# A two-layer gated cross-attention kernel: layer 0 projected once a batch, its stacks taken through a scratch in HBM

## The chip, the cores and the metric

One core of a Trainium2 chip runs the whole kernel in one launch. The metric is the device time of one execution in microseconds (us). The kernel before took 320.93 us, the median of 3 runs (319.45 to 321.24).

## What is computed

x is 2 batches of 256 tokens of 128 values, ctx is 2 batches of 512 tokens of 128 values. Four residual steps, each gated by a tanh of a learned number:

```
x = x + tanh(g_xattn[0]) * attention0(layernorm(x), ctx)   # 16 heads of 8, shared mask
x = x + tanh(g_ffn[0])   * quantised_linear(layernorm(x))  # x @ Hadamard, 4 bit, ternary weights
x = x + tanh(g_xattn[1]) * attention1(layernorm(x), ctx)   # 16 heads of 64, mask by batch
x = x + tanh(g_ffn[1])   * moe(layernorm(x))               # 32 experts, top 4, one shared expert
```

Each attention projects queries, keys and values, takes a masked softmax of the scores over 512 keys, mixes the values and projects out. All inputs are float32, and the scores must keep float32 accuracy. The router picks experts by rank, so small errors upstream matter. That is why queries and keys are split into a high part and a low remainder, and products of both parts are added up.

## The kernel before, in words

**Units, blocks and slots.** A unit is one head and 128 queries of one batch: a 128x512 tile of scores. Layer 0 has 8 blocks (2 batches x 4 groups) of 8 units (4 heads x 2 query tiles); layer 1 has 16 blocks (2 batches x 8 groups) of 4 units. Units are numbered 0 to 127. Every engine runs the same written order over slots t from -6 to 129, each its own part: TensorE computes in slot t the scores of unit t+6, then the jobs planned for t, the mix and output projection due in t, and turns (transposes) unit t; VectorE masks unit t+5, takes the reciprocal of unit t+3, evicts the jobs of slot t-1 and copies half of the turned tiles; ScalarE takes the exponential of unit t+4 and copies the other half; GpSimd normalises unit t+3. There is no reordering: an instruction that waits holds up all behind it on its engine. From slot 130 the experts follow.

**Jobs.** `make_plan` (line 105) says in which slot a projection or another piece of side work is issued, `BEFORE` what comes ahead of slot -6. Jobs take two PSUM banks in turn, and a job waits until the last user of its bank was evicted (`freed`).

**Layer 0's projections.** Each of the 8 blocks projects its own k (L991), q (L988) and values (L995). The weights are laid out so that 32 columns, four heads of 8, stand four times over the 128 output rows. One eviction on ScalarE (L577) and one on VectorE (L762) leave the high parts in some row groups and the low parts in the others, so that one matmul over 128 rows (L1057) adds all four products. The k stack is then ready. The q stack is copied once per head by GpSimd (`q_stack`, L453 to L460), multiplied by 1 in the rows of that head and by 0 in the others. Values are copied into 8 of every 32 columns (L735).

**Mix and output.** When a block's 8 units are turned, TensorE mixes them with the values (L1089) into `mix_bank`, ScalarE copies it with its bias (L556), and two matmul pairs (L1101) add it into `y_bank`. That is once for each of the 8 blocks.

**The feed-forward's chain** (`feed_forward`, L812) starts when a batch's last output projection is in, at slot `Y_DONE[0, b]` (37 and 69), and goes through all engines in steps o = 0 to 17 behind that slot: residual add, statistics, 1/sqrt on GpSimd, normalise, turn (o = 4), rotate (7), quantise (9, 10), turn (11), linear (13), add (14), statistics, normalise, turn (17). Layer 1's first q (slot 55 for batch 0) needs its result. The weights' ternary form (`ternary`, nine VectorE operations) is made in slots -4 to -2.

**Layer 1's stacks.** k and q of a block are stacked by DMAs from SBUF to SBUF that SyncE issues in plan order (`stack_k` L395, 4 DMAs; `stack_q` L403, 6 DMAs), each pair behind the slot of its projection. Scores of layer 1 (L1063, L1064) wait for them. SyncE also loads the experts' weights there (L424).

**Loads.** All inputs are loaded at the start, SyncE's in the order of L378 to L391.

Of the kernel before, what the change touches and what calls it, by code (L numbers as in the profile page):

```python
# [53 lines left out]
for _name, _n in (("bq0", 4), ("bk0", 4), ("bq1", 8), ("bk1", 8), ("gates", 4), ("lo_k", 1), ("lo_q", 1),  # L54
                  ("head_row", 4), ("neg_half", 4), ("bv0", 4), ("bv1", 8)):
    COL[_name], NCOLS = slice(NCOLS, NCOLS + _n), NCOLS + _n
# [48 lines left out]
def make_plan():  # L105


    before = [("k", 0), ("ln", 0, 0), ("q", 0), ("v", 0)]
    plan = {}
    ahead = ({"k": 13, "q": 11, "v": 10}, {"k": 13, "q": 11})  # L110
    for k in BLOCKS[1:]:
        for name, slots in ahead[k.layer].items():
            if name == "q" and k.layer == 1 and k.g == 0:
                slots = 9
            plan.setdefault(k.first - slots, []).append((name, k.m))
# [3 lines left out]
    plan.setdefault(4, []).append(("turn_fw",))  # L119
# [19 lines left out]
    for j in order:  # L139
        if j[0] in ("k", "q"):  # L140
            count += 1
            highs[j] = count
# [19 lines left out]
PIECES_FROM = 14  # L162

# [12 lines left out]
def build(nc, a, out):  # L176
    ctx = ExitStack()
    with ctx:
# [21 lines left out]
        head_row, gates = cols[:, COL["head_row"]], cols[:, COL["gates"]]  # L200
# [5 lines left out]
        ctxT = sb("ctxT", [P, NC * P])  # L206
# [25 lines left out]
        w0T = shared[:, 0:2048].rearrange("p (g i c) -> p g i c", g=4, i=4)  # L232
        stack_f = shared[:, 2048:2304]
        mask0 = shared[:, 2304:2816].bitcast(BF16).rearrange("p (t k) -> p t k", t=NQ)
        we3 = shared[:, 0:HALVES * P].rearrange("p (e c) -> p e c", e=HALVES)
        parts = sb("parts", [P, 3840], F32R)
        q0 = parts[:, 0:2048].rearrange("p (i h q) -> p i h q", i=2, h=4)
        k0 = parts[:, 2048:3072].rearrange("p (i k) -> p i k", i=2)
        high_k, high_q = parts[:, 3072:3584], parts[:, 3584:3840]
        w1_late = parts[:, 0:3072].rearrange("p (g n i c) -> p g n i c", g=4, n=2, i=3)  # L240
        gateT = parts[:, 3072:3584]
        minus_bq0 = sb("minus_bq0", [P, 4])
        minus_bk0 = sb("minus_bk0", [P, 4])
        bo0 = sb("bo0", [P, P])
        m0_u8 = sb("m0_u8", [P, NQ, SK], U8)
# [13 lines left out]
        k1_both = sb("k1_both", [P, NKQ, 2, SK], F32R)  # L259
# [985 lines left out]
```

## Time and profile before

| | us |
|---|---|
| median of 3 runs | 320.93 |
| the profiled execution | 321.6 |
| its span, first to last instruction | 319.9 |
| TensorE busy | 281.8 (88%) |
| VectorE busy | 226.1 (71%) |
| ScalarE busy | 197.6 (62%) |
| GpSimd busy | 132.9 (42%) |

The profile records one execution. PE is TensorE, PEld its weight loads, DVE VectorE, ACT ScalarE, POOL GpSimd, SP SyncE; SPq is a DMA issue on SyncE. L12 is line 12 of the kernel. Times are us from the span's start. Ends of matmuls are modelled, so starts are the better measure: the cost of a TensorE instruction in a busy stretch is the start of the next one less its own.

### The profile page before, as it was taken

To read this page: it belongs to the slowest core of one execution; us is meant where nothing else is said; L and a number is where in the kernel's file an instruction comes from. 1 tells how busy PE (TensorE), PEld (TensorE's weight loads), DVE (VectorE), ACT (ScalarE), POOL (GpSimd) and SP (SyncE) were. 2 spreads that over 40 slices of the span, in tenths; PEclk is the share of its full clock that TensorE was granted. 3 is DMA by queue.
4 is the path that set the end of the run, shared out by engine and by line. 5 is a ranking of instruction groups with operands and counts; after the bars stand their busy time and mean duration, and the time that the engine had idled before them with its cause. 6 is when DMAs were issued, how large, how long until landed. Compare 5 with 4: busy or idle time off the path is not lost.

```text
span 319.9 us, 6774 instructions
## 1 busy us (share of the span) xinstructions
PE 281.8 (88%) x1963; PEld 218.1 (68%) x1963; DVE 226.1 (71%) x713; ACT 197.6 (62%) x475; POOL 132.9 (42%) x209
## 2 busy tenths in 40 slices
PE   2649799999778759999999999999999789989996
PEld 0426476677466537688877788888787558777995
DVE  1489887897785956788789677797786117376653
ACT  1258698898685756797776666676967642613221
POOL 4436768876775552748453233343244000000000
PEclk9999999999997998999999999999999799979999
DMA  6900000000000253545456367665620000000000
GB/s 186 395 6 1 3 0 2 4 0 1 3 0 2 66 121 95 141 116 127 115 143 172 95 157 203 172 179 152 169 59 3 0 2 1 0 2 16 1 2 16
DMA packets 17124, 23.43 MB, mean 73 GB/s; under 512 B 3264, under 2 KB 10944, under 8 KB 16960
## 3 DMA queue, kind: packets, MB, share of 16 engines
q1 hardware_dynamic: 16656, 22.64, 25.7%
q10 hardware_dynamic: 432, 0.35, 0.6%
q8 instruction: 17, 0.28, 0.4%
q14 instruction: 19, 0.16, 0.1%
HBM read 8.04 MB, written 0.26 MB: 26 GB/s over the span
## 4 chain that ended last, share of the span: by engine, by line
PE 57%; DVE 17%; issue 10%; ACT 5%; DMA 4%; POOL 3%; SPq 3%; DVEq 0%; ACTq 0%; POOLq 0%
PE bank L1089 13%; PE bank L951 12%; PE bank L1131 4%; PE bank L1152 4%; PE bank L1155 4%; DVE masked L705 4%; PE bank L1063 3%; PE bank L1064 3%; PE bank L1057 2%; POOL probs L451 2%; SPq L409 2%; PE bank L1101 2%; DVE probsT L721 2%; DMA q<-q_split 2%; PE bank L956 2%
## 5 line engine op out<-in xcount | busy, mean ns | idle before, releaser
L451 POOL TENSOR_SCALAR probs<-probs,rsum 128x512 f32<-128x512 f32 x128 | 88.4, 695 | 104.8 <-DVE rsum L714 104.2
L540 ACT ACTIVATE probs<-masked,neg_max 128x512 f32<-128x512 f32 x128 | 91.8, 719 | 7.2 <-DVE neg_max L705 7.2
L951 PE MATMUL bank<-ident,probs 128*128 128x128 f32 x512 | 79.7, 279 | 3.3 <-ACT probsT L548 1.7
L951 PEld LDWEIGHTS bank<-ident,probs 128*128 128x128 f32 x512 | 59.4, 143 | 22.7 <-issue 13.7
L705 DVE CUSTOM_DVE_ANT_0 masked<-bank,mask 128x512 f32<-128x512 f32 x64 | 43.7, 683 | 17.0 <-PE bank L1064 13.9
L548 ACT ACTIVATE probsT<-bank 128x512 f32<-128x512 f32 x74 | 43.7, 591 | 17.8 <-PE bank L951 17.7
L1089 PE MATMUL bank<-probsT,val 128*32 128x256 f32 (+1 forms) x512 | 49.4, 405 | 1.3 <-ACT mixT L556 1.3
L721 DVE COPY probsT<-bank 128x512 f32<-128x512 f32 x54 | 36.7, 679 | 19.3 <-PE bank L951 19.2
L705 DVE CUSTOM_DVE_ANT_0 masked<-bank,shared 128x512 f32<-128x512 f32 x64 | 43.3, 678 | 1.4 <-PE bank L1057 1.2
L1089 PEld LDWEIGHTS bank<-probsT,val 128*32 128x32 f32 (+1 forms) x512 | 25.6, 128 | 21.0 <-issue 8.9
L1057 PE MATMUL bank<-parts 128*128 128x512 f32 x64 | 31.1, 492 | 8.7 <-issue 6.5
L651 ACT ACTIVATE probsT<-bank 128x256 f32<-128x256 f32 x34 | 13.0, 385 | 36.9 <-PE bank L1152 36.9
L1063 PE MATMUL bank<-k_high,q 128*128 128x512 f32 x64 | 30.5, 477 | 3.9 <-DMA q<-q_split 3.9
L935 DVE TENSOR_TENSOR probsT<-bank,probsT 128x256 f32<-128x256 f32 x32 | 13.6, 424 | 22.3 <-PE bank L1155 11.1
L1064 PE MATMUL bank<-k_both,q 128*128 128x512 f32 x64 | 25.2, 394 | 0.0
L540 ACT ACTIVATION_READ_ACCUMULATOR probs<-masked,neg_max 128x1 f32 x128 | 24.9, 194 | 0.0
L556 ACT ACTIVATE mixT<-bank,cols 128x256 f32<-128x256 f32 x24 | 11.3, 472 | 17.4 <-PE bank L1089 17.3
L1131 PE MATMUL bank<-we,probsT 128*128 128x128 f32 x136 | 21.2, 280 | 0.1
L714 DVE RECIPROCAL rsum<-sums 128x1 f32<-128x1 f32 x128 | 19.9, 156 | 1.7 <-ACT probs L540 1.7
L1057 PEld LDWEIGHTS bank<-parts 128*128 128x128 f32 x64 | 12.4, 195 | 12.8 <-issue 11.8
L1152 PE MATMUL bank<-xnT,w_flat 128*128 128x256 f32 x68 | 20.9, 390 | 0.0
L1155 PE MATMUL bank<-xnT,shared 128*128 128x256 f32 x68 | 20.8, 388 | 0.0
(166 smaller groups left out, 470.9 us busy)
## 6 DMA issues: line engine op xcount, KB each, us to landing
q<-q_split SPq DMA_DIRECT2D x96, 64.0 KB, 2.0
k_both<-k_low SPq DMA_DIRECT2D x32, 128.0 KB, 2.9
k_both<-k_high SPq DMA_DIRECT2D x32, 128.0 KB, 3.2
w_flat<-in_w SPq DMA_DIRECT2D x1, 1536.0 KB, 9.7
shared<-in_w0T SPq DMA_DIRECT2D x1, 768.0 KB, 7.1
w_flat<-in_we SPq DMA_DIRECT2D x2, 384.0 KB, 3.6
shared<-in_we SPq DMA_DIRECT2D x2, 384.0 KB, 4.2
we<-in_we SPq DMA_DIRECT2D x2, 384.0 KB, 4.4
```

The source lines that it names most:

```text
L451: pool.tensor_scalar(p, p, rsum[:, u % NCOL:u % NCOL + 1], 1.0, ALU.mult, ALU.mult).then_inc(normed, 1)
L540: act.activation(probs[:, u % NP, :], masked[:, u % NS, :], ACT.Exp, scale=-1.0, bias=neg_max[:, c:c + 1], accum_out=sums[:, c:c + 1]).the ...
L548: act.activation(probsT[:, k.m % 2, h, :, qt * P:qt * P + P], turn_bank[u % 2][:, :].rearrange("p (k q) -> p k q", q=P), ACT.Copy).then_in ...
L705: dve.tensor_tensor_reduce(out=masked[:, u % NS, :], in0=score_bank[u % 2][:, :], in1=mask, scale=-float(k.depth) ** -0.5, scalar=3.0e38, ...
L721: dve.tensor_copy(probsT[:, k.m % 2, h, :, qt * P:qt * P + P], turn_bank[u % 2][:, :].rearrange("p (k q) -> p k q", q=P)).then_inc(copied[ ...
L951: ins = pe.transpose(dst[0:rows, t * P:t * P + P], src, ident[:, :])
L1057: pe.matmul(dst, q0[:, i, h, q], k0[:, i, :], start=True, stop=True).then_inc(scored, 1)
L1063: pe.matmul(dst, q1_high[:, s, h, q], k1_high[:, s, :], start=True, stop=False)
L1064: pe.matmul(dst, q1_both[:, s, h, q], k1_both[:, s, h, :], start=False, stop=True).then_inc(scored, 1)
L1089: ins = pe.matmul(mix_bank[w * h:w * h + w, 0:SQ], v[:, i, w * h:w * h + w], probsT[:, k.m % 2, h, i, :], start=(i == 0), stop=(i == NK - 1))
L1131: ins = pe.matmul(moe_bank[b][:, t * P:t * P + P], hidT[:, n % 2, t * P:t * P + P], we2[:, p, :], start=(p == 0 and t == 0), stop=(p == PA ...
L1152: pe.matmul(u_bank[i][:, 0:SQ], we1[:, p, :], xT, start=True, stop=True).then_inc(u_ready, 1)
```

## The change

- **Layer 0 is projected once a batch.** New jobs `kn`, `qn` and `v0` project all 16 heads in one go: one k, q and value projection for each batch. The split is as in layer 1: high part by ScalarE, low part by VectorE. Block 0 alone is still projected in the repeated layout (from `w00T`), so that it needs no DMA; its q is put into the four heads' tiles by four VectorE operations on 32 partitions each, in place of GpSimd's `q_stack`.
- **Stacks go through HBM.** SyncE writes the high and low parts to `staged_k` and `staged_q` in HBM, each row twice, waits, and reads them back as the stacks of blocks 1 to 7: one DMA for k and four for q in each block. Rows now alternate high and low inside a head. There are four stack buffers in place of two, cleared once by GpSimd.
- **Mixes are summed over groups.** The values of group g stand in the columns of g, zeros elsewhere, and the four blocks of a batch add into one `mix_bank`. Copy and output projection come once a batch.
- **The chain takes 15 steps**: residual add and statistics in o = 0, normalise 2, turn 3, rotate 5, quantise 7 and 8, turn 9, linear 11, add 12, statistics 13, normalise 14, turn 15. Layer 1's first q of each batch comes two slots sooner (53 and 85).
- **Moved**: the ternary weights to slots 11 to 13 (turned in 18, before 4), the loads of layer 1 behind the stacks of blocks 1 to 3. Layer 1's q stack takes 4 DMAs (a repeated source) in place of 6. Expert loads wait also for the context's split, since the context now lies in `shared`.

```diff
-    before = [("k", 0), ("ln", 0, 0), ("q", 0), ("v", 0)]
-    plan = {}
-    ahead = ({"k": 13, "q": 11, "v": 10}, {"k": 13, "q": 11})
-    for k in BLOCKS[1:]:
-        for name, slots in ahead[k.layer].items():
-            if name == "q" and k.layer == 1 and k.g == 0:
-                slots = 9
-            plan.setdefault(k.first - slots, []).append((name, k.m))
+    before = [("k", 0), ("kn", 0), ("ln", 0, 0), ("q", 0), ("qn", 0)]
+    plan = {1: [("v0", 0)]}
+    for k in BLOCKS[8:]:
+        plan.setdefault(k.first - 13, []).append(("k", k.m))
+        plan.setdefault(k.first - 11, []).append(("q", k.m))
+    for n, name in enumerate(("kn", "qn", "v0")):
+        plan.setdefault(LN01_AT + 7 + n, []).append((name, 1))
-        for o, job in ((4, ("ln", 1, b)), (7, ("rotate", b)), (11, ("turn_xq", b)), (13, ("ffn", b)),
-                       (17, ("ln", 2, b))):
+        for o, job in ((3, ("ln", 1, b)), (5, ("rotate", b)), (9, ("turn_xq", b)), (11, ("ffn", b)),
+                       (15, ("ln", 2, b))):
...
+            def stage_k0(b):
+                sp.wait_ge(*freed(("kn", b)))
+                for low, src in ((0, k1_high[:, b, :]), (1, k1_low[:, b, :])):
+                    sp.dma_start(staged_k[b, :, low::2, :].bitcast(F32),
+                                 src.bitcast(F32).unsqueeze(1).to_broadcast([P, 2, SK])).then_inc(k_staged[b], 16)
+                sp.wait_ge(k_staged[b], 32)
+
+            def stage_q0(b):
+                sp.wait_ge(*freed(("qn", b)))
+                for low in range(2):
+                    sp.dma_start(staged_q[b, :, 2 * low:2 * low + 2, :].bitcast(F32),
+                                 q1_split[:, b, low, :].bitcast(F32).unsqueeze(1).to_broadcast([P, 2, SQ])).then_inc(q_staged[b], 16)
+                sp.wait_ge(q_staged[b], 32)
+
+            def stack_k0(k):
+                i, c = k.m % 4, 32 * k.g
+                if k.m >= 4:
+                    sp.wait_ge(scored, BLOCKS[k.m - 4].end)
+                sp.dma_start(k0[:, i, :].bitcast(F32),
+                             staged_k[k.b, c:c + 32, :, :].bitcast(F32).rearrange("c j k -> (c j) k")).then_inc(stacked0[i], 16)
+
+            def stack_q0(k):
+                i, c = k.m % 4, 32 * k.g
+                if k.m >= 4:
+                    sp.wait_ge(scored, BLOCKS[k.m - 4].end)
+                for h in range(4):
+                    sp.dma_start(q0[32 * h:32 * h + 32, i, h, :].bitcast(F32),
+                                 staged_q[k.b, c + 8 * h:c + 8 * h + 8, :, :].bitcast(F32)
+                                 .rearrange("c j q -> (c j) q")).then_inc(stacked0[i], 16)
+
+            stage_k0(0)
+            for k in BLOCKS[1:4]:
+                stack_k0(k)
+            stage_q0(0)
+            sp.wait_ge(late_ready, 2)
+            for k in BLOCKS[1:4]:
+                stack_q0(k)
             sp.dma_start(m1_u8[:, :, :, :], a["mask1"]).then_inc(ld["m1"], 16)
             sp.dma_start(w1_flat[:, :], a["w1"]).then_inc(ld["w1"], 16)
...
+            stage_k0(1)
+            stage_q0(1)
+            for k in BLOCKS[4:8]:
+                stack_k0(k)
+                stack_q0(k)
...
-                    for copy in range(2):
-                        sp.dma_start(q1[own[h], s, h, copy, :].bitcast(F32),
-                                     q1_split[own[h], i, 0, :].bitcast(F32)).then_inc(q_stacked[s], 16)
+                    sp.dma_start(q1[own[h], s, h, :, :].bitcast(F32),
+                                 q1_split[own[h], i, 0, :].bitcast(F32).unsqueeze(1).to_broadcast([64, 2, SQ])).then_inc(q_stacked[s], 16)
...
+                            sp.wait_ge(ctx_split, 2 * B)
...
+                        for h in range(4):
+                            r = slice(32 * h, 32 * h + 32)
+                            ins = dve.scalar_tensor_tensor(out=q0[r, 0, h, :], in0=job_bank[r, 0:SQ], scalar=bq00[r, 0:1],
+                                                           in1=high_q[r, :].bitcast(F32), op0=ALU.add, op1=ALU.add)
+                            ins.then_inc(q0_ready if h < 3 else free, 1)
...
+                    else:
+                        pe.wait_ge(stacked0[k.m % 4], 80 * turns_of_stack0(k.m))
+                    pe.matmul(dst, q0[:, k.m % 4, h, q], k0[:, k.m % 4, :], start=True, stop=True).then_inc(scored, 1)
...
-                                        probsT[:, k.m % 2, h, i, :], start=(i == 0), stop=(i == NK - 1))
+                                        probsT[:, k.m % 2, h, i, :], start=(first and i == 0), stop=(last and i == NK - 1))
...
-                if t in (-4, -3, -2):
-                    ternary(t + 4)
+                if t in (11, 12, 13):
+                    ternary(t - 11)
```

## Rows read from the trace of the kernel before

**Rows 1.** The page's busy line: us, share of the span, instructions.

```profile
PE 281.8 (88%) x1963; PEld 218.1 (68%) x1963; DVE 226.1 (71%) x713; ACT 197.6 (62%) x475; POOL 132.9 (42%) x209
```

**Rows 2.** Stretches: from:to, length, busy us of each engine, granted clock, DMA share, GB/s.

```profile
25.80:76.10 50.30, 47.25 (x376) 33.88 (x375) 42.59 (x144) 41.46 (x104) 37.19 (x62) 1.00 0.01 2
60.05:70.90 10.85, 10.60 (x93) 7.75 (x96) 9.19 (x32) 9.25 (x24) 8.40 (x15) 1.00 0.01 2
76.10:110.50 34.40, 26.84 (x202) 19.44 (x201) 28.06 (x98) 24.73 (x61) 21.05 (x33) 0.95 0.07 16
110.50:117.50 7.00, 3.63 (x24) 2.97 (x24) 4.72 (x14) 4.61 (x11) 5.26 (x8) 1.00 0.27 66
117.50:133.80 16.30, 15.82 (x114) 12.03 (x118) 11.45 (x34) 10.30 (x25) 6.80 (x11) 0.90 0.51 122
192.00:200.00 8.00, 8.00 (x59) 6.42 (x58) 6.01 (x18) 5.56 (x14) 2.91 (x5) 1.00 0.75 202
```

**Rows 3.** TensorE's timeline, unit 8 and a steady block: start, us, what.

```profile
25.78 0.47 PE L1057 MATMUL bank<-parts 128*128 128x512 f32 x1
...
49.12 1.93 PE L1089 MATMUL bank<-probsT,val 128*32 128x256 f32 x32
...
51.71 1.02 PE L991 MATMUL bank<-ctxT,shared 128*128 128x512 f32 x2
52.57 0.60 PE L951 MATMUL bank<-ident,probs 128*128 128x128 f32 x4
...
55.58 1.05 PE L995 MATMUL bank<-shared,ctxT 128*128 128x128 f32 x8
56.47 0.60 PE L951 MATMUL bank<-ident,probs 128*128 128x128 f32 x4
```

**Rows 4.** VectorE's timeline in that block.

```profile
51.67 0.69 DVE L721 COPY probsT<-bank 128x512 f32<-128x512 f32 x1 [1.24 <-PE bank L951]
...
58.80 0.67 DVE L705 CUSTOM_DVE_ANT_0 masked<-bank,shared 128x512 f32<-128x512 f32 x1
...
59.47 0.67 DVE L721 COPY probsT<-bank 128x512 f32<-128x512 f32 x1
60.05 0.68 DVE L705 CUSTOM_DVE_ANT_0 masked<-bank,shared 128x512 f32<-128x512 f32 x1
```

**Rows 5.** Groups of VectorE instructions: busy us, mean ns, then idle before.

```profile
L762 DVE SCALAR_TENSOR_TENSOR parts<-bank,cols,parts 128x512 fp32r<-128x512 f32 x8 | 6.0, 749 | 4.4 <-ACT parts L577 3.8 <-PE bank L1057 0.6
L762 DVE SCALAR_TENSOR_TENSOR shared<-bank,cols,parts 128x256 f32<-128x256 f32 x8 | 3.8, 472 | 2.5 <-ACT parts L577 2.5
L735 DVE COPY val<-bank 128x128 f32<-128x128 f32 x8 | 2.2, 272 | 0.6 <-PE bank L995 0.6
L799 DVE TENSOR_REDUCE fcol<-fw 128x1 f32<-128x128 f32 x1 | 0.3, 276 | 0.0
L810 DVE TENSOR_TENSOR fq<-fw,fs 128x128 f32<-128x128 f32 x1 | 0.5, 450 | 0.0
```

**Rows 6.** The start, TensorE's and GpSimd's timelines.

```profile
6.38 2.04 PE L991 MATMUL bank<-ctxT,shared 128*128 128x512 f32 x2 [6.38 <-DMA ctxT<-in_ctxT]
...
13.80 1.84 POOL L459 TENSOR_SCALAR parts<-shared,cols 128x256 fp32r<-128x256 f32 x4 [4.11 <-DVE shared L762]
```

**Rows 7.** DMAs (KB, us to landing), then layer 1's first q stack and the waits.

```profile
q<-q_split SPq DMA_DIRECT2D x96, 64.0 KB, 2.0
out<-x_sb SPq DMA_DIRECT2D x2, 128.0 KB, 1.8
...
115.32 0.60 SPq L411 DMA_DIRECT2D q<-q_split  x1
...
117.48 0.47 PE L1063 MATMUL bank<-k_high,q 128*128 128x512 f32 x1 [2.98 <-DMA q<-q_split]
...
118.11 3.19 PE L1089 MATMUL bank<-probsT,val 128*32 128x256 f32 x32
...
133.08 0.47 PE L1063 MATMUL bank<-k_high,q 128*128 128x512 f32 x1 [0.48 <-DMA q<-q_split]
```

More of the change, by code:

```diff
@@ L162, with mixes, turns_of_stack0 @@
 PIECES_FROM = 14
+VALUES_AT = {4: (0, (0, 1, 2, 3)), 20: (1, (0,)), 22: (1, (1,)), 29: (1, (2,)), 37: (1, (3,))}
+def mixes(k):
+    return k.b + 1 if k.layer == 0 else k.m - 5
+def turns_of_stack0(m):
+    return m // 4 + (1 if m % 4 else 0)
 def turns_of_stack(m):
@@ L278, in build @@
         lr = sb("lr", [P, NQ])
-        ex = sb("ex", [P, NQ, EXPERTS])
-        sc = sb("sc", [P, NQ, EXPERTS])
         top8 = sb("top8", [P, NQ, 8])
-        above = sb("above", [P, NQ, EXPERTS])
-        equal = sb("equal", [P, NQ, EXPERTS])
-        run = sb("run", [P, NQ, EXPERTS])
         room = sb("room", [P, NQ])
-        sel = sb("sel", [P, NQ, EXPERTS])
         sel_b = sb("sel_b", [P, NT, EXPERTS], BF16)
-        kept = sb("kept", [P, NQ, EXPERTS])
-        wgt = sb("wgt", [P, NQ, 2, EXPERTS])
+        ex, sc, above, equal, run, sel, kept = (small[:, 64 * i:64 * i + 64].rearrange("p (t e) -> p t e", t=NQ) for i in range(7))
+        wgt = small[:, 4 * P - 64:5 * P - 64].rearrange("p (t i e) -> p t i e", t=NQ, i=2)
         ones32 = sb("ones32", [P, EXPERTS])
@@ L336, in build @@
         ctx_split = sem("ctx_split")
+        k_staged = [sem("k_staged0"), sem("k_staged1")]
+        q_staged = [sem("q_staged0"), sem("q_staged1")]
+        stacked0 = [sem(f"stacked0_{i}") for i in range(4)]
+        val_ready = sem("val_ready")
         w1_split = sem("w1_split")
@@ L451, in norm @@
                 pool.tensor_scalar(p, p, rsum[:, u % NCOL:u % NCOL + 1], 1.0, ALU.mult, ALU.mult).then_inc(normed, 1)
-            def q_stack(m):
-                pool.wait_ge(*freed(("q", m)))
-                if m >= 2:
-                    pool.wait_ge(scored, BLOCKS[m - 2].end)
-                for j in range(4):
-                    pool.tensor_scalar(q0[:, m % 2, j, :], stack_f[:, :], head_row[:, j:j + 1], 1.0,
-                                       ALU.mult, ALU.mult).then_inc(q0_ready, 1)
             splits = [0]
@@ L494, in _ @@
                     norm(t + LEAD - 3)
-                for job in PLAN.get(t - 1, ()):
-                    if job[0] == "q" and BLOCKS[job[1]].layer == 0:
-                        q_stack(job[1])
+                if t in VALUES_AT:
+                    b, groups = VALUES_AT[t]
+                    for g in groups:
+                        values(b, g)
                 if t in SPLIT_AT:
@@ L621, in attend @@
                 for k in BLOCKS:
-                    if t == k.copy_at:
+                    if t == k.copy_at and (k.layer or k.g == 3):
                         mix_copy(k)
@@ L1076, in mix @@
                 if k.layer == 0:
-                    pe.wait_ge(*freed(("v", k.m)))
-                    v = val[:, k.m % NV, :, :]
+                    pe.wait_ge(val_ready, k.m + 1)
+                    v = val[:, k.g, :, :]
+                    first, last = k.g == 0, k.g == k.groups - 1
                 else:
@@ L1083, in mix @@
                     v = val1[:, two % NV1, :, odd * P:odd * P + P]
-                if k.m >= 1:
-                    pe.wait_ge(mix_copied, k.m)
+                    first = last = True
+                if first and k.m:
+                    pe.wait_ge(mix_copied, mixes(k) - 1)
                 w = k.width
@@ L1118, in attend @@
                         mix(k)
-                    if t == k.out_at:
+                    if t == k.out_at and (k.layer or k.g == 3):
                         project_out(k)
```

249 lines of the change are left out of this document (138 added, 111 removed).

## The prediction

> **What bounds the kernel now.** The kernel works in slots t: in slot t TensorE computes the scores of unit t+6 and turns unit t, VectorE masks unit t+5, and each engine keeps its written order. I read the page's busy line first [rows 1]: TensorE is busy 88% of the span, VectorE 71%. That is a mean over unlike stages, so the second view is the table of stretches [rows 2]. In a steady block of layer 0 (60.05 to 70.90, 8 units in 10.85 us) TensorE is busy 10.60 and VectorE 9.19, so TensorE ends it. In the stretch with batch 0's feed-forward chain (76.1 to 110.5) TensorE is busy only 26.84 of 34.4 and VectorE 28.06: there the chain, which is mostly VectorE work, ends it, and TensorE waits in order. In layer 1 (192 to 200) TensorE is busy 8.00 of 8.00. The change touches layer 0 and the chain, so only the time up to about 117 us and two small waits behind it can move.
>
> Third comes TensorE's timeline of one block [rows 3]. Behind each row the reader subtracts its start from that of the next instruction. One k projection costs 0.86 (51.71 to 52.57), the values 0.89 (55.58 to 56.47), the mix 1.9 by its own duration. I put q, with half of k's columns, at 0.43 and an output projection, half as many matmuls as the values, at 0.44; both are estimates. Fourth is VectorE's timeline [rows 4]: mask plus reciprocal take 0.67 (58.80 to 59.47), a turned copy 0.58 (59.47 to 60.05). With a copy in every other unit that is 0.96 a unit, 7.7 a block. The copy at 51.67 waited 1.24 behind the mix, once a block. So without the projections VectorE (7.7 plus 1.2) and TensorE (10.60 less 2.6 of jobs) are both near 8 to 9: VectorE is what is late next.
>
> **The change, part by part.** All sums run against the profiled execution (321.6 us, span 319.9 and 1.7 around it). The median of the runs is 0.7 lower.
>
> A, the start. Before, scores of unit 8 (block 1, slot 2) start at 25.78 [rows 3]. After, block 1 needs its stack from the scratch. The first k pair of matmuls took 2.04 from 6.38 [rows 6]; the new full k projection is another such pair, to 10.5; its eviction on ScalarE (about 0.7) and its low part on VectorE (0.75, like the parts row of [rows 5]) free it at 12.0. Then SyncE issues, in order: two staging DMAs of k (1.05 MB in sum, each row written twice), waits for them, three k stacks (0.79 MB), two staging DMAs of q (0.52 MB), waits, and four q stacks before block 1 is complete. An issue takes 0.6 and a small transfer lands 2.0 after its issue begins [rows 7]. For the rate the nearest row is 192 to 200: 202 GB/s at a DMA share of 0.75 [rows 2], so 270 GB/s full. k is staged at 12.0 + 2.0 + 3.9 = 17.9; q behind the k stacks at 17.9 + 2.0 + 4.9 = 24.8; the fourth q stack starts at 26.6 and lands at 28.6. Scores of unit 8 start at 29.0: **+3.2**. Bounds: at 202 GB/s it is 32 (+6); if bytes cost nothing the stack lands at 22.8 and VectorE's eight masks end near 22 as well, so 23 (-3). I take 270, since these packets are like the ones in that row. What is queued behind SyncE's two waits are the mask and weight loads of layer 1. The mask is wanted in slot 12 and the weights in slot 22 at the earliest, 10 us and more after they are issued at about 32. The first query's four heads were four GpSimd operations (1.84 in all from 13.80 [rows 6]); now they are four VectorE operations on 32 partitions, 0.4 to 0.47 each by the q row of [rows 5]. Mask 0 starts some 0.7 later, inside A's wait. GpSimd's memsets grow by about 1.8 us and lie ahead of its first normalisation: nothing.
>
> The Trainium skill (DMA: Bandwidth & Descriptors, Anatomy of one DMA) speaks against A: a fixed cost of about 2.0 us per DMA, mostly the receipt of the last write, "surprisingly long" where the target is HBM, plus bytes at 436 GB/s. Our only writes to HBM are the two stores of the result, and they landed in 1.8 us against 2.0 for SBUF to SBUF [rows 7], so the trace shows the fixed part and no surcharge. By the page's two figures unit 8 would start about 1.5 us earlier than by mine.
>
> B, slots 2 to 37 (before 25.8 to 76.1, 50.3 us). VectorE was busy 42.6. It loses five k (0.75), four q (0.47) and five v copies (0.27) [rows 5], 7.0 in sum; it gains the full k and q low parts of batch 1 (0.75 + 0.47), two value copies of a full bank (0.68 each, as the copy rows of [rows 4]), and the nine ternary operations moved from slots -4 to -2 into 11 to 13 (3.2; first and last of nine in [rows 5]), 5.8 in sum. That leaves 41.4 busy. Four mixes at 1.24 of idle each give 46.4: **-3.9**. Below, TensorE's own sum would allow 38; above, nothing saved. I take VectorE's sum, the later of the two. The ternary move costs its 3.2 here because A's wait would have covered it and slot 11 doesn't. GpSimd loses 32 operations of 0.49 for eight small copies, ScalarE five k and five q evictions and three mix copies: both were no bound.
>
> Batch 1's stack: its k is projected in slot 13 (about 44), freed at 46, and by A's path with one k stack in place of three it lands near 60. Block 4 is wanted in slot 26, near 62. Slack 2 us: taken as nothing, and the first thing to go.
>
> C, the chain (slots 37 to 55, 34.4 us; after 37 to 53). VectorE's busy 28.06 loses the jobs of the two blocks in it (one k, two q, two v: 2.2) and two slots at 0.96 (1.9): 23.9. Its idle time of 6.3 loses the two waits of 0.6 for k's eviction: 5.1. Together 29.0: **-5.4**. The chain's steps themselves (quantise, normalise) are untouched, about 10 us on VectorE. Bounds: -2.2 if the cut slots only stretch the others, -8 if the idle time goes too.
>
> D, from q to the first scores of layer 1. Before 7.0 us over three slots, TensorE busy 3.63 [rows 2]: SyncE issued six DMAs, the last at 115.32, and TensorE idled 2.98 [rows 7]. After there are four, and five slots. DMAs alone: 1.7 to the first issue, 1.8, 2.0, so 5.5; five slots take about 6.5. **-0.5**, the stall turned into work that C already counts. Bounds -1.5 and +1.
>
> E, the clock. In the 16.3 us behind that stall the granted clock is 0.90 [rows 2], and the mix took 3.19 against 1.93 in the steady block [rows 3, 7]. Without the stall that is **-1.2**. The new idle stretch in A will bring such a dip too, but VectorE sets the pace there. The Trainium skill (TensorE: Matmul & The Clock Gate, HAM oscillation) has the same rule, idle gaps bring the half rate back; by it A's gap is the one to fear, and with half-rate work for one mix behind it the sum would be 1.2 higher.
>
> F, layer 1. Two more waits for q stacks, 0.48 at 133.08 [rows 7] and the like at 183; the first has four DMAs in place of six, batch 1's q comes two slots (4 us) sooner. **-0.9**, bounds 0 and -1.5. The expert loads now also wait for the context's split in slot 80, which holds SyncE up for up to three slots, while block 15's stack is wanted in slot 86: nothing.
>
> Sum: 3.2 - 3.9 - 5.4 - 0.5 - 1.2 - 0.9 = -8.7, so 312.9 beside 321.6, and **312.2** beside the median.
>
> **The rivals.** R1, TensorE stays the bound throughout. For: it was, in steady blocks [rows 2]. Behind unit 8 it loses five k, five q, five v and six output projections: 4.3 + 2.2 + 4.5 + 2.6 = 13.6. This takes the place of B and C: 3.2 - 13.6 - 0.5 - 1.2 - 0.9 = -13.0, near 308. Against: VectorE's sum in B, and TensorE's idle 7.6 us in the chain.
>
> R2, the three engines hand one another too many short waits once none has slack, and half of B, C, E and F is lost while A and D stand: 3.2 - 5.7 - 0.5 = -3.0, near 318. For: between 25.8 and 76.1 TensorE, the bound, was still idle for 3 us (47.25 busy of 50.3) [rows 2]. Against: six units of lead.
>
> R3, the other side: the scratch is the new wait. If the path from freed k to complete stack takes x longer than my 17 us, A grows by x and block 4's wait by x - 2. The change is slower from 2x - 2 > 8.7, x above 5.4. At x = 9 it costs +7.3, near 328. For: nothing in the trace stores 1 MB to HBM or reads it back at once; two waits stand in one queue. Against: loads at the start land fast and the two stores in 1.8 us.
>
> R4, the shorter chain doesn't do what it says: the same work in fewer slots just makes each slot longer, and C gives -3.5. Near 314, inside the forecast's range.
>
> **How the numbers follow.** Forecast (with R4) 0.59, R1 0.15, R2 0.17, R3 0.09. R1 and the forecast are faster by over 0.5% (1.6 us, about what a measurement of this kernel can tell from no change); R2 nearly always, 0.14 of its 0.17; R3 splits 0.01 same, 0.08 slower. Faster 0.88, same 0.04, slower 0.08. The range runs from 306 (R1, with A's lower bound in part) to 319 (R2).
>
> **What would show it.** A: scores of unit 8 at 27 to 32, with an idle TensorE ahead of them waiting for a DMA. B: a steady block near 8.9 us instead of 10.85, VectorE the busiest. C: 28 to 31 us from the first residual add to q of layer 1. D, E: no 3 us wait before layer 1's first scores, the mix behind it under 2 us. F: those two waits gone. The prediction is wrong if unit 32 waits for its stack, if a steady block stays over 10 us, or if the stretch behind 133 moves by more than 2 us.

## The result and the profile after

| | before | after |
|---|---|---|
| median, us (range, runs) | 321.09 (319.45 to 323.26, 4) | 310.87 (309.31 to 311.81, 4) |
| ratio to before, 95% interval | 1 | 0.9673 (0.9603 to 0.9743) |
| profiled execution, us (span) | 321.6 (319.9) | 310.97 (309.2) |
| granted clock, mean | 0.979 | 0.972 |

The changed kernel is 10.2 us faster; 312.2 was predicted, range 306 to 319. The same kernel, timed again later (e12), gave 311.05 (6 runs), ratio 0.9708 (0.9663 to 0.9753). Ratios leave out executions over 1.5% above the fastest of their kernel, medians keep them, so the two can differ by some thousandths.

The page's busy line of the kernel after, beside [rows 1]: TensorE lost 13.3 us of work, VectorE 2.2.

```profile
PE 268.5 (87%) x1871; PEld 206.8 (67%) x1871; DVE 223.9 (72%) x700; ACT 190.1 (61%) x459; POOL 124.3 (40%) x187
```

Stretches of the kernel after, columns as in [rows 2]. In order: unit 8 to the first residual add (50.30 us before, 47.35 now), a steady block (10.85, now 8.90), the chain (34.40, now 28.40), q to the first scores of layer 1 (7.00, now 7.20), and the piece behind them, whose clock was 0.90 and is 1.00. The mean clock column of the first and the third line is below 1.00: TensorE ran at its lower level for a part of them. In the steady block VectorE (7.10) and TensorE (8.40) both have gaps; neither is full.

```profile
25.95:73.30 47.35, 41.17 (x323) 28.69 (x323) 40.12 (x139) 35.26 (x88) 29.95 (x50) 0.96 0.38 125
60.30:69.20 8.90, 8.40 (x73) 5.78 (x72) 7.10 (x25) 6.46 (x18) 5.14 (x9) 1.00 0.36 97
73.30:101.70 28.40, 20.68 (x166) 15.25 (x163) 24.37 (x85) 20.02 (x51) 16.82 (x25) 0.94 0.00 1
101.70:108.90 7.20, 5.03 (x34) 4.17 (x34) 6.63 (x21) 6.67 (x18) 5.36 (x9) 1.00 0.68 147
108.90:122.50 13.60, 13.60 (x109) 10.75 (x109) 10.70 (x31) 8.96 (x22) 7.70 (x11) 1.00 0.65 142
```

TensorE's timeline of the kernel after, the instructions that answer to [rows 3] and [rows 7] and those with the longest waits (in brackets, with their releaser). Unit 8 starts at 25.95, as before, but behind a DMA; unit 32 (59.92) waits for its stack; the first scores of layer 1 still wait 1.67; and in layer 1 there is a new wait of 1.38 at batch 1's turned query (149.40).

```profile
25.95 0.66 PE L1134 MATMUL bank<-parts 128*128 128x512 f32 x1 [2.26 <-DMA parts<-staged_q]
...
59.92 0.47 PE L1134 MATMUL bank<-parts 128*128 128x512 f32 x1 [1.24 <-DMA parts<-staged_q]
60.32 1.93 PE L1168 MATMUL bank<-probsT,val 128*32 128x256 f32 x32
...
101.68 0.35 PE L1024 MATMUL bank<-x_high,w_early 128*128 128x256 f32 x1 [1.23 <-DVE x_low L813]
108.88 0.47 PE L1140 MATMUL bank<-k_high,q 128*128 128x512 f32 x1 [1.67 <-DMA q<-q_split]
109.51 1.93 PE L1168 MATMUL bank<-probsT,val 128*32 128x256 f32 x32
...
131.51 0.50 PE L1140 MATMUL bank<-k_high,q 128*128 128x512 f32 x1 [0.70 <-DVE neg_max L767]
136.96 0.44 PE L1019 MATMUL bank<-ident,xn 128*128 128x128 f32 x2 [0.38 <-DVE k_low L843]
149.40 0.41 PE L1019 MATMUL bank<-ident,xq 128*128 128x128 f32 x2 [1.38 <-DVE xq L862]
```

Where the 10.7 us between the two profiled spans went. A milestone is the start of a unit's scores or of a slot's mix, read from the two TensorE timelines.

| stretch | before | after | difference | forecast |
|---|---|---|---|---|
| start to unit 8 | 25.78 | 25.95 | +0.2 | +3.2 |
| unit 8 to scores of slot 37 | 49.98 | 47.33 | -2.6 | -3.9 |
| to q of layer 1 | 34.8 | 28.4 | -6.4 | -5.4 |
| to unit 64 | 6.95 | 7.20 | +0.2 | -0.5 |
| to the mix of slot 66 | 16.2 | 13.6 | -2.6 | about -1.5 |
| to the mix of slot 94 | 59.8 | 61.7 | +1.9 | about -0.5 |
| to the end | 126.4 | 125.0 | -1.4 | 0 |

The forecast's E (-1.2) and F (-0.9) are spread over the last three lines.

### The profile page after: what moved, and what is told of

Its sections match the earlier page's. It is cut to its first block, busy times and chain, and to the rows that moved or that the text cites. A ratio compares the mean times of both kernels' runs of the same rounds, so it can differ in the third digit from the quotient of the medians.

```text
span 309.2 us, 6506 instructions
## 1 busy us (share of the span) xinstructions
PE 268.5 (87%) x1871; PEld 206.8 (67%) x1871; DVE 223.9 (72%) x700; ACT 190.1 (61%) x459; POOL 124.3 (40%) x187
## 4 chain that ended last, share of the span: by engine, by line
PE 59%; DVE 14%; DMA 9%; issue 7%; ACT 5%; POOL 3%; SPq 3%; DVEq 0%; ACTq 0%; POOLq 0%
PE bank L1019 13%; PE bank L1168 12%; PE bank L1212 5%; PE bank L1233 4%; PE bank L1140 4%; PE bank L1236 4%; PE bank L1141 4%; DMA staged_q<-q_split 3%; DMA staged_k<-k_low 3%; PE bank L1024 2%; PE bank L1134 2%; PE bank L1026 2%; PE bank L1025 2%; PE bank L1181 2%; PE bank L1242 2%
## 5 line engine op out<-in xcount | busy, mean ns | idle before, releaser
L1019 PE MATMUL bank<-ident,probs 128*128 128x128 f32 x512 | 80.8, 282 | 2.9 <-DVE probsT L783 1.3
L1019 PEld LDWEIGHTS bank<-ident,probs 128*128 128x128 f32 x512 | 60.9, 144 | 19.8 <-issue 9.3
L1168 PE MATMUL bank<-probsT,val 128*32 128x256 f32 (+1 forms) x512 | 46.6, 384 | 1.3 <-ACT mixT L616 1.3
L1134 PE MATMUL bank<-parts 128*128 128x512 f32 x64 | 33.5, 529 | 11.9 <-DVE neg_max L767 7.9
L1168 PEld LDWEIGHTS bank<-probsT,val 128*32 128x32 f32 (+1 forms) x512 | 24.6, 123 | 19.3 <-issue 5.2
L1003 DVE TENSOR_TENSOR probsT<-bank,probsT 128x256 f32<-128x256 f32 x32 | 13.6, 424 | 21.8 <-PE bank L1236 11.5
L1134 PEld LDWEIGHTS bank<-parts 128*128 128x128 f32 x64 | 13.1, 206 | 18.2 <-DVE neg_max L767 13.4
L1212 PEld LDWEIGHTS bank<-we,probsT 128*128 128x128 f32 x136 | 18.7, 196 | 0.7 <-DVE probsT L1008 0.3
```

The source lines that it names most:

```text
L1019: ins = pe.transpose(dst[0:rows, t * P:t * P + P], src, ident[:, :])
L1134: pe.matmul(dst, q0[:, k.m % 4, h, q], k0[:, k.m % 4, :], start=True, stop=True).then_inc(scored, 1)
L1168: ins = pe.matmul(mix_bank[w * h:w * h + w, 0:SQ], v[:, i, w * h:w * h + w], probsT[:, k.m % 2, h, i, :], start=(first and i == 0), stop=( ...
L1212: ins = pe.matmul(moe_bank[b][:, t * P:t * P + P], hidT[:, n % 2, t * P:t * P + P], we2[:, p, :], start=(p == 0 and t == 0), stop=(p == PA ...
```

## The experiments

Ratios are to the kernel before, with 95% intervals; the changed kernel stands at 0.9673 and 0.9708. The edit of e3 is made to the kernel before, all others to the changed kernel. No run puts layer 0's projections back into the changed kernel, so what they are worth by themselves is read from the traces and not tried.

**The chain: 17 steps again, in both batches and in batch 1 only; and 15 steps in the kernel before.** `LONG` is (0, 1) in e1 and (1,) in e2; the projection of the batch's first q moves back with it. e3 is the reverse edit on the kernel before.

```diff
-        for o, job in ((3, ("ln", 1, b)), (5, ("rotate", b)), (9, ("turn_xq", b)), (11, ("ffn", b)),
-                       (15, ("ln", 2, b))):
+        for o, job in (((4, ("ln", 1, b)), (7, ("rotate", b)), (11, ("turn_xq", b)), (13, ("ffn", b)),
+                        (17, ("ln", 2, b))) if b in LONG else
...
-                if o in (7, 8):
-                    quantise(b, o - 7)
+                q_at = 9 if long else 7
+                if o in (q_at, q_at + 1):
+                    quantise(b, o - q_at)
```

> The changed kernel with the feed-forward's chain back at 17 steps in both batches, everything else as changed. Theory: in layer 0 the 15-step chain saves about two slots (2 us) between the residual add and q of layer 1, but in layer 1, where slots take 2 us anyway, it only makes TensorE wait in order for VectorE (1.38 us ahead of the turn of xq, 0.38 ahead of the layernorm turn), some 2 us. So undone in both batches it is about even: 310 to 312, with scores of unit 64 near 111 (after 108.9) and layer 1's blocks from slot 66 to 94 in 60 us in place of 61.7. Rival: the shorter chain is worth its two slots in both batches; then 314 to 315.

> The changed kernel with the chain at 17 steps for batch 1 alone. Theory: keeps layer 0's gain and takes back layer 1's loss: 309 (2 us under the changed kernel's 310.9), unit 64 still at 108.9, no wait over 0.5 us ahead of the turn of xq near 150. Rival: layer 1's loss has nothing to do with the chain's steps (the denser stacks, the clock): then 311, and the wait for the q stack of block 16 comes back for 0.5 us more.

> The kernel before with the 15-step chain alone. Theory: in layer 0 it saves two slots and the 3 us wait ahead of unit 64 (3 to 4 us at unit 64: 114), and loses 2 us in layer 1: near 319. Rival: as VectorE still has the projections' evictions, the slots only stretch and nothing is saved in layer 0: 321 to 323.

Measured: e1 311.98, 0.9677 (0.9648 to 0.9706); e2 308.59, 0.9573 (0.9546 to 0.9600); e3 322.39, 1.0010 (0.9972 to 1.0048). So the cut as a whole is worth nothing that can be measured: e1 equals the changed kernel, and e3 came out as its rival said. It costs in batch 1. Mix of slot 66 to mix of slot 94, first the kernel before, then e3, e1 and e2, each from its own trace:

```profile
133.70:193.50 59.80, 59.02 (x432) 46.30 (x431) 48.28 (x148) 42.17 (x102) 29.61 (x46) 1.00 0.54 138
```

```profile
134.60:196.20 61.60, 59.00 (x432) 46.26 (x431) 48.22 (x147) 42.35 (x102) 29.59 (x46) 1.00 0.53 137
```

```profile
123.30:182.90 59.60, 59.09 (x434) 46.35 (x433) 48.96 (x151) 42.78 (x104) 29.89 (x46) 1.00 0.59 142
```

```profile
123.20:182.40 59.20, 58.89 (x432) 46.28 (x431) 48.87 (x151) 42.84 (x104) 29.89 (x46) 1.00 0.59 143
```

And the changed kernel:

```profile
122.40:184.10 61.70, 59.13 (x432) 46.30 (x431) 48.89 (x151) 43.08 (x104) 30.06 (x46) 1.00 0.58 137
```

TensorE's work is 59 us in all five. With 17 steps it is idle for 0.3 to 0.8 in sum; with 15, for 2.6. The three waits at 131.51, 136.96 and 149.40 (2.46 together) are that: TensorE reaches its turns before VectorE has masked, quantised and split. In e3 the same wait stands in the kernel that has nothing else of the change:

```profile
161.48 0.41 PE L950 MATMUL bank<-ident,xq 128*128 128x128 f32 x2 [1.38 <-DVE xq L793]
```

Batch 0 is less clear. Between e1 and e2, which differ only there, the times differ by 0.0104 of 321, 3.3 us, but the profiles reach unit 64 together (109.73 and 109.68; e2 was expected at 108.9) and slot 94 within 0.4; most of the rest of their spans' difference (309.5 and 307.4) lies in the last stretch, where e1 had a clock of 0.90 between 229.6 and 247.4. From the mix of slot 34 to unit 64, the changed kernel, then e1, then e2:

```profile
69.20:108.90 39.70, 29.81 (x247) 22.46 (x246) 34.07 (x116) 29.67 (x76) 25.08 (x38) 0.96 0.13 28
```

```profile
68.10:109.70 41.60, 31.38 (x246) 22.05 (x245) 33.95 (x116) 30.28 (x77) 25.27 (x38) 0.96 0.11 25
```

```profile
68.10:109.70 41.60, 32.21 (x247) 24.50 (x246) 34.30 (x116) 29.64 (x76) 24.74 (x37) 0.88 0.12 25
```

Here e1 and e2 are equally long for different reasons. In e2 TensorE's work slows between 78.48 and 81.91 (four turned tiles 1.06 in place of 0.60, scores 0.77 in place of 0.48), behind a wait of 1.46; the changed kernel has the same wait and doesn't slow. That block takes e2 13.76 (68.15 to 81.91) and the changed kernel 12.13 (69.22 to 81.35). In three more profiles with 15 steps in batch 0 the stretch takes 40.4 (e12), 39.7 (e5b) and 39.6 (e6b). So batch 0's cut gains 1 to 2 us in its own stretch where the clock doesn't take it back, on the strength of one profile with 17 steps. In the kernel before the stretch takes 46.6 at a clock of 0.96, and 48.0 with 15 steps at 0.89, so that pair doesn't speak against it. One profile of each kernel doesn't tell what gave e2's 3.3 us.

**The scratch: everything stored twice, one after the other.** In e4 each staging stores first to a spare scratch and waits for it.

```diff
             def stage_k0(b):
                 sp.wait_ge(*freed(("kn", b)))
+                for low, src in ((0, k1_high[:, b, :]), (1, k1_low[:, b, :])):
+                    sp.dma_start(spare_k[b, :, low::2, :].bitcast(F32),
+                                 src.bitcast(F32).unsqueeze(1).to_broadcast([P, 2, SK])).then_inc(spare[b], 16)
+                sp.wait_ge(spare[b], 32)
```

> The changed kernel with each staging of k and q done once more ahead, into a spare scratch, with its wait. Theory: the way through HBM is on the path at unit 8 and at unit 32 (TensorE waited 2.26 and 1.24 us there): k's second staging adds about 4 us and q's about 4 to 5, so unit 8 moves from 25.95 to about 34 and unit 32 waits another 8: 325 to 328. Rival: VectorE has work in store behind the wait and makes up most of it; then 313 to 318.

Measured: 327.74, 1.0170 (1.0134 to 1.0205): slower than the kernel before. Two waits in e4's TensorE timeline, units 8 and 32:

```profile
33.80 0.77 PE L1146 MATMUL bank<-parts 128*128 128x512 f32 x1 [8.79 <-DMA parts<-staged_q]
...
74.99 0.77 PE L1146 MATMUL bank<-parts 128*128 128x512 f32 x1 [8.17 <-DMA parts<-staged_q]
```

Unit 8 is 7.9 us later, and unit 32 another 7.2 on top of that (15.1 against 59.92). Nothing hides the path to the scratch, in either batch: R3's mechanism is real. By an estimate from these numbers (a gain of 10.2 us, two batches) the change would be worth nothing with each round trip some 5 us longer; e4's are 7 to 8 us longer.

**The query's staging ahead of the wait for the key's.** e5b issues both stagings before it waits for either.

```diff
             def stage_k0(b):
...
-                sp.wait_ge(k_staged[b], 32)
...
+            stage_q0(0)
+            sp.wait_ge(k_staged[0], 32)
```

> The changed kernel with q's staging issued as soon as q is free, ahead of the k stacks and of the wait for k's staging, in both batches. Theory: unit 8 waits for the q stack of block 1, whose staging was issued 1.3 us late and moved behind 0.8 MB of k stacks: unit 8 at 23.6 in place of 25.95, and unit 32's wait of 1.24 us goes. Sum -3 us at unit 64 at best, VectorE's work behind unit 8 gives part of it back: 308 to 310. Rival: bytes in flight decide, not their order; unit 8 stays near 26 and the time at 311.

Measured: 307.24, 0.9586 (0.9516 to 0.9656), some 3 us faster than the changed kernel and a little better than expected. SyncE's issues of the changed kernel (issue time, us, what), and then of e5b:

```profile
12.60 0.62 SPq L405 DMA_DIRECT2D staged_k<-k_low  x1
16.49 1.29 SPq L420 DMA_DIRECT2D parts<-staged_k  x3
17.82 0.94 SPq L412 DMA_DIRECT2D staged_q<-q_split  x2
22.79 5.44 SPq L428 DMA_DIRECT2D parts<-staged_q  x12
```

```profile
16.97 0.90 SPq L411 DMA_DIRECT2D staged_q<-q_split  x2
...
20.33 5.45 SPq L426 DMA_DIRECT2D parts<-staged_q  x12
```

The q stacks are issued 2.5 us sooner: 0.85 because q's staging is issued sooner, 1.6 because it takes 3.36 from its issue in place of 4.97. It is tempting to put the 1.6 down to the 0.8 MB of k stacks that are in flight ahead of it in the changed kernel, but batch 1's q staging, issued at 50.31 with nothing before it still under way, took 4.91 there too; e4's second stores of the same data took 2.9. What sets this time is open. Unit 8 starts at 23.98 (2.0 earlier), without a wait for a DMA, and the wait at unit 32 is gone; the mix of slot 34 comes at 65.31 in place of 69.22. The order of the two waits in one queue cost this.

**The ternary operations back into the start.**

```diff
-                if t in (11, 12, 13):
-                    ternary(t - 11)
+                if t in (-4, -3, -2):
+                    ternary((-4, -3, -2).index(t))
```

> The changed kernel with the nine ternary operations back in slots -4 to -2, as before. Theory: they stand there on VectorE between the first masks, in time that unit 8's wait covers; the slots 11 to 13 lose 3.2 us of VectorE work, and the first steady block shrinks from 13.5 to about 10.5 us: 308 to 309. Rival: TensorE and ScalarE are as close to the bound, 310 to 311.

Measured: 308.06, 0.9626 (0.9549 to 0.9703). The block with slots 11 to 18, in the changed kernel and in e6b:

```profile
36.40:49.90 13.50, 11.45 (x88) 7.72 (x87) 12.24 (x41) 9.83 (x24) 7.24 (x12) 1.00 0.22 80
```

```profile
37.00:48.10 11.10, 10.62 (x89) 7.75 (x89) 9.81 (x33) 9.27 (x24) 7.22 (x12) 1.00 0.26 97
```

VectorE's busy time falls by 2.43 and the block by 2.40: one for one. In the start it is not quite free (the block begins 0.6 later). The times agree with 2 to 3 us, though their intervals overlap the changed kernel's. These operations are no part of what TensorE waits for unit by unit, so it is VectorE's time in its order that counts.

**Is TensorE still the bound? The mixes per block again (e7b), and 28 score matmuls twice (e8b).** Both only add work: e7b copies and projects the context of every group, e8b repeats every other unit's scores.

```diff
-    return k.b + 1 if k.layer == 0 else k.m - 5
+    return k.m + 1
...
-                    if t == k.out_at and (k.layer or k.g == 3):
+                    if t == k.out_at:
```

```diff
+                    if k.m and u % 2:
+                        pe.matmul(dst, q0[:, k.m % 4, h, q], k0[:, k.m % 4, :], start=True, stop=True)
```

> The changed kernel with the mix copied and projected out for every block of layer 0 again (6 ScalarE copies and 6 pairs of output projections more), summed in y as before. Theory (VectorE sets the pace in layer 0): TensorE and ScalarE have room, less than 1 us slower, 311 to 312. Rival (TensorE is still the bound): 6 x 0.44 us of projections are added one for one, 313.5.

> The changed kernel with the scores of every second unit from 9 to 63 computed twice by TensorE into the same bank: 28 matmuls of 0.32 us, 9 us of TensorE work, no other engine has more. Theory: with VectorE the bound of layer 0, most of it is hidden in TensorE's idle time (6.2 us between 25.95 and 73.3, 7.7 in the chain): 312 to 314. Rival (TensorE the bound): 318 to 320.

Measured: e7b 309.96, 0.9680 (0.9604 to 0.9756); e8b 310.79, 0.9714 (0.9615 to 0.9813), both cheaper than even the theory had it. Summing the mixes over groups is worth nothing that can be measured. One of e8b's added matmuls costs 0.23 from its start to that of the next instruction:

```profile
51.69 0.39 PE L1136 MATMUL bank<-parts 128*128 128x512 f32 x1
51.92 0.60 PE L1019 MATMUL bank<-ident,probs 128*128 128x128 f32 x4
```

So 28 of them are 6.5 us (the expectation said 9). The page's busy time is no measure of this: it is 273.3 (e8b) and 272.2 (e7b) against 268.5 and 269.6 in two profiles of the changed kernel, but kernels with just the changed kernel's TensorE work lie between 266.9 (e5b) and 272.8 (e9). The stretch between the mixes of slots 10 and 34, changed kernel and then e8b:

```profile
36.41:69.22 32.81, 28.50 (x233) 19.33 (x232) 28.02 (x97) 25.71 (x65) 20.90 (x34) 1.00 0.31 98
```

```profile
35.54:68.14 32.60, 30.58 (x244) 21.30 (x244) 28.25 (x98) 25.73 (x66) 21.05 (x35) 1.00 0.33 101
```

Twelve more matmuls, 2.8 us by their starts, and the same time. A part of them went into the wait for the stack at unit 32 (1.24 in the changed kernel, 0.56 here); with these waits taken off, the stretches are 31.6 and 32.0, so about a sixth of the added work shows. By R1, where TensorE's work is the time, e8b would be 6.5 us slower. The intervals of the totals leave room for 3 to 4, so R1 is out for layer 0; e7b, with 2.6 us of work, couldn't have told by its total.

**The same with VectorE: 14 masks twice.**

```diff
+                if k.layer == 0 and k.m and u % 4 == 1:
+                    step(dve.tensor_tensor_reduce(out=masked[:, u % NS, :], in0=score_bank[u % 2][:, :], in1=mask,
+                                                  scale=-float(k.depth) ** -0.5, scalar=3.0e38, op0=ALU.add, op1=ALU.min,
+                                                  accum_out=neg_max[:, c:c + 1]))
```

> The changed kernel with the mask operation of every fourth unit from 9 to 61 done twice by VectorE into the same tile: 14 operations of 0.61 us and a short wait for the first, some 9 to 9.5 us of VectorE work, as much as the doubled scores gave TensorE. Theory (VectorE sets the pace of layer 0 behind unit 8): nearly all of it is added, 318 to 320. Rival (neither engine does, the waits from one to the other do): as cheap as the doubled scores, 311 to 313.

Measured: 318.34, 0.9948 (0.9880 to 1.0016); the changed kernel, on the same chip, 311.05, so +7.3. The same stretch of e9:

```profile
37.37:73.59 36.22, 29.33 (x233) 19.39 (x232) 31.81 (x108) 25.55 (x64) 20.56 (x34) 0.99 0.28 88
```

VectorE's busy time is 3.8 longer and the stretch 3.4, though the wait of 1.24 at unit 32 is gone. It is plainest in a steady block, e5b's (which has no wait for a stack) and then e9's:

```profile
56.42:65.31 8.89, 8.37 (x73) 5.78 (x72) 7.86 (x29) 7.92 (x21) 6.54 (x11) 1.00 0.23 71
```

```profile
52.86:63.22 10.36, 8.61 (x73) 5.76 (x73) 9.16 (x33) 7.97 (x22) 7.71 (x14) 1.00 0.53 165
```

A doubled mask takes 0.73 (56.02 to 56.75 in e9); two a block are 1.46, and the block is 1.47 longer. Over the whole kernel VectorE's busy time is 9.6 more (233.5 against 223.9) for 7.3 of time; behind unit 64 TensorE's wait for the q stack is 0.26 in place of 1.67, so a part is absorbed there as well. In a steady block of layer 0 a microsecond of VectorE costs one; one of TensorE costs a sixth to a quarter (e8b: four matmuls, 0.9 more, and 9.12 for 8.90, from 59.02 to 68.14).

**Put together.** e10 is e5b, e2 and the ternary operations in the start (two of three behind batch 0's key, the third in slot -2); e11 also projects block 8's key two slots earlier; e12 is the changed kernel again.

```diff
+                if j[0] == "kn":
+                    ternary(0)
+                    ternary(1)
...
-        plan.setdefault(k.first - 13, []).append(("k", k.m))
+        plan.setdefault(k.first - (15 if k.m == 8 else 13), []).append(("k", k.m))
```

> The changed kernel with three edits whose single gains were 3.6, 2.8 (3.4 by ratio 0.9573 against 0.9673) and 2.8 us: q's staging issued first, the chain of batch 1 at 17 steps, the ternary weights off slots 11 to 13 (two of three parts in VectorE's idle time ahead of the first q, the last in slot -2). Theory: the three act in different places, so their gains add up but for the part of the ternary gain that unit 8's wait covered: 302 to 304. Rival: what one gives back another takes again at the same wait (unit 32 or unit 64), 305 to 307.

> The three edits, and the k projection of block 8 in slot 49 in place of 51, so that its four stack DMAs are done before those of q. Theory: the wait for the q stack ahead of unit 64 (1.1 to 1.7 us) is DMA transfers of k and q side by side (DMA share 0.68 between 101.7 and 108.9, the last q stack took 3.4 us to land): it goes or halves, 1 us faster than the three edits alone. Rival: SyncE's issue of q's four DMAs and one landing are the way, whatever k does: the same time.

> The changed kernel as it is, for comparison on the same chip: 310 to 312.

Measured: e10 305.94, 0.9541 (0.9487 to 0.9595); e11 304.30, 0.9471 (0.9412 to 0.9530); e12 311.05, 0.9708 (0.9663 to 0.9753). Both beat either kernel: e11 by 5% and 2.2%. The gains don't add, as e10's rival said. In e10's trace unit 8 is back at 26.37 and the mix of slot 34 comes at 65.61, where e5b alone had 65.31. Of the 2.4 at unit 8, 1.3 is there at the score ahead of it (23.38 for 22.07), where TensorE had waited 1.24 for a mask behind the ternary operations of slot -2; the other 1.1 is TensorE's own work at half its rate (the values 1.91 at 23.95, in e5b 1.15 at 22.64; e10's clock column says 1.00 there, but these durations don't). With the stack's arrival no longer setting unit 8, work at the start costs. What is left of e10's gain over e5b is batch 1's chain: 59.5 in place of 61.7 between the mixes of slots 66 and 94, less 0.8 that it loses between the mix of slot 34 and unit 64. Whether e11's own edit does anything is open: its interval overlaps e10's, and TensorE's wait ahead of unit 64 is 1.03 against 1.08 (e11's trace is of its longest execution, 306.96).

## Why the prediction was right, step by step

The time was right, within 1.4 us, and half of its terms were off, in both directions. Of its signs, a steady block of 8.9, a chain of 28 to 31 us, no wait of 3 us ahead of layer 1's first scores and the end of the two q waits came true. Unit 8 came ahead of the stated 27 to 32; VectorE was not the busiest in a steady block; and one sign of being wrong was met: unit 32 waited for its stack.

**A, the start: sized wrongly, +0.2 for +3.2.** The mechanism was there (an idle TensorE of 2.26 ahead of unit 8, waiting for the stack). k is staged at 16.47 (forecast 17.9), q at 22.77 (24.8), and the stack is complete at 25.82 (28.6): 13.9 us from freed k in place of 16.6. The chain of the kernel after (start, us, what; lines left out between them):

```profile
12.60 3.87 DMA staged_k<-k_low
...
18.29 4.48 DMA staged_q<-q_split
...
24.10 1.72 DMA parts<-staged_q
```

I had charged the bytes at 270 GB/s on top of a full 2.0 us. An issue took 0.42 to 0.47 on SyncE for the small stacks (5.44 for twelve), not 0.6. The Trainium skill (DMA: Bandwidth & Descriptors, Anatomy of one DMA) gives about 2.0 us fixed and warns of HBM as the target; its figures are for DMAs issued by GpSimd, and these are SyncE's. The 32 KB stack took 1.72. For 1 MB the page's two figures make an estimate of 4.4 from the first issue; the trace has 4.5 (11.94 to 16.47). Here the page was nearer than my rate, and its warning cost nothing that can be seen. The prediction also did this sum wrong: by these figures 1.05 MB take 1.5 us less than at my rate, but the 1.31 MB of k stacks and q behind them another 1.9, so the estimate is unit 8 at 25.6, 3.4 us earlier and not 1.5. Measured was 25.95.

k was free at 11.94 for a forecast of 12.0, and that was luck. The first loads landed 1.8 sooner than before (VectorE's first instruction at 4.63, before 6.45), and GpSimd's memset, which the forecast put at nothing, seems to have held VectorE up for 2.4 (last section). What the trace calls idle depends on TensorE as well: in e12 the stack came at the same time (unit 8 at 25.84), but TensorE had worked at half its rate ahead of it and idled for only 0.57.

**B, layer 0: right but for one wait.** The steady block took 8.90, as forecast. The -2.6 includes 1.24 at unit 32; without it -3.9, the forecast. In e5b's undisturbed blocks (8.90 and 8.89) VectorE is busy 7.8 and 7.9 and idles 1.13 and 1.03 behind the mix, nearly the forecast's 7.7 and 1.24; TensorE shows more, 8.4, and still e8b and e9 confirm that VectorE's work is what the block takes. The ternary move costs 2.4 of the 3.2 (e6b).

I had called unit 32's slack 2 us and "the first thing to go", and it went. From freed k to complete stack it took 13.95 (45.84 to 59.79), the forecast's 14, and slots 13 to 26 took 17.6 where I had allowed 18 (41.0 to the 58.7 at which TensorE came for it). What was off lies ahead of both: with unit 8 three microseconds early, k was projected at 41.37 and not at 44, but it was free only 4.5 us later and not 2. ScalarE had its high part by 43.1; VectorE came to the low part at 45.10, behind masks and the ternary operations. So the need came 3.3 sooner and the stack 0.2. In e6b, without the ternary operations there, the staging is issued 2.6 behind the projection (41.21 to 43.77) and the wait is 0.60.

**C, the chain: -6.4 for -5.4.** I gave 1.9 of it to the two slots cut. e1 restores them and loses 1 to 2 us there, but nothing in the total; the kernel before gains nothing from the cut (e3). VectorE's busy time fell by 3.7, [rows 2] against 24.37, for the forecast 4.2; its idle time by 2.3, from 6.3 to 4.0, for 1.2. The two waits of 0.60 for k's eviction are gone, as forecast; the rest is above all one wait behind a mix, 3.15 at 103.44 before (the mix itself took 2.55) and 0.40 at 98.00 now. R4, that slots only get longer, was not met: a slot of this stretch takes 1.78 with 15 steps and 1.75 with 17 (e1, 31.55 for 18), before 1.93.

**D: +0.2 for -0.5.** TensorE still waits 1.67. The last of the q DMAs is issued at 105.30 and takes 3.44 to land, where I used 2.0. The DMA share is 0.68 in that stretch, against 0.27 in [rows 2]: k stacks of layer 1 travel beside it.

**E, the clock: right in place, larger.** With a wait of 1.67 in place of 2.98 the mix behind it takes 1.93 in place of 3.19 and the clock is 1.00; unit 64 to slot 66 is 2.6 shorter, of which 0.48 is F's. The wait in A did bring a dip, as the prediction said: from 25.95 to 29.50 the clock was 0.52, and four turned tiles took 1.05 in place of 0.60. By the Trainium skill (TensorE: Matmul & The Clock Gate, HAM oscillation) an idle gap brings the half rate back. The traces agree, but the length of one gap doesn't tell: ahead of unit 64 gaps of 1.67, 1.83 (e12) and 2.05 (e1) were followed by a mix of 1.93, one of 1.85 (e3) by a mix of 2.90, and one of 2.98 (before) by 3.19.

**F, layer 1: the step that failed, +1.9 for about -0.5.** The prediction said that layer 1 gains from two q stacks that come sooner. The waits of 0.48 and 0.44 for q stacks did go, but the 15-step chain of batch 1 put 2.46 of in-order waits into TensorE, which is otherwise full there. I priced the shorter chain where VectorE sets the pace and not where TensorE does. e2 takes it away: 2.5 us less in this stretch, 2.3 in the medians, 3 to 4 by the ratios.

**The end: -1.4, not forecast.** Around the last scores of layer 1, from 240 to 258, the kernel before has a granted clock of 0.91, and its last three mixes are 7.3 and 4.7 apart (246.07, 253.39, 258.06); after it is 1.00, with 6.5 and 3.8 (236.70, 243.24, 247.05). That is 1.6, a little more than all of it. Both kernels have the same waits there (0.8, 1.1 and 1.3 for ScalarE); the rate behind the first two differs (four turned tiles 1.06, now 0.60). e1 has the slow form again (7.3), e3 in part (7.0), and all the others 6.5. Nothing tried here accounts for it, and whether it is chance stays open. The errors of A (-3.0) and of the end (-1.4) are cancelled by those of B, D and F (+1.3, +0.7, +2.4), so that what is left, 2 us, is that of C and E: partly luck.

R2 (halved gains) is out: nothing in layer 0 was halved. R3 was not met: the path was 2.7 us shorter than my sum, and it needed to be over 5 us longer; e4 shows what it costs when it is.

## What to carry to other kernels

Price a shorter pipeline stage by stage: where the engine that does the chain's work set the pace, the cut gained 1 to 2 us, and where another engine was full, it made that one wait in its order and cost as much. For a round trip through HBM, try putting every store whose data is ready ahead of the first wait in that queue; here this took the path off unit 8 and unit 32. Which engine still counts after a change is asked by doubling a small operation on each, not read from busy shares, and what the doubled operation adds is read from the starts of the instructions around it. A clock dip can hide or feign a gain of 1 to 2 us in a single profile, so compare the clock of a stretch before its length.

## What the runs showed of the hardware

VectorE's normalisation at the start took longer beside a GpSimd memset. VectorE's timeline of the kernel after, then GpSimd's in the same time:

```profile
6.76 3.84 DVE L746 TENSOR_SCALAR xn<-x_sb,mv,rstd 128x128 f32<-128x128 f32 x2 [0.91 <-POOL rstd L503]
```

```profile
7.80 2.66 POOL L537 MEMSET parts<- 128x3072 f32 x1
```

Before, the same two VectorE instructions took 1.43, beside a GpSimd operation of 1.04; now the first takes 0.79 and the second, begun just behind the memset, ends 0.14 after it. The Trainium skill (SBUF — State Buffer, SBUF: two separate sides) calls the port pair that VectorE and GpSimd share an exclusive lock, and the trace looks like it. It was not tried apart. The key's evictions on VectorE start at 10.52, right behind; ScalarE had the high part of the whole key ready at 9.12. By an estimate from these rows an earlier memset might bring the staging forward by some 2 us.

Stores to HBM that are read back at once showed no surcharge against the kernel's other transfers: 3.87 for the second half of a 1 MB staging, the same in both batches, and 1.72 and 2.78 for a 32 KB stack read back. The second half of a 0.5 MB staging took 4.48 behind 0.8 MB of loads and 4.47 with none ahead of it, longer than the 3.87 of twice the bytes; e5b and e4 show that it can be quicker (the whole staging in 3.36 and 2.9 us, not 4.9), and no run shows why.
